# Nine small index tables of the feed-forward part are declared behind the large buffers instead of ahead of them

## The reference

```python
x = x + xattn(ctx, ctx, layernorm(x), ssm_kernel, D, 8)   # 64 heads, causal convolution of length 1024
h = layernorm(x).reshape(-1, 1024)                         # 8192 tokens
scores = sigmoid(h @ router_w)                             # 32 experts, 8 are taken per token
...
gate = ragged_dot(xs, w_gate, group_sizes)                 # (1024 -> 512) per expert
up   = ragged_dot(xs, w_up, group_sizes)
down = ragged_dot(silu(gate) * up, w_down, group_sizes)    # (512 -> 1024)
routed = (down[unsort].reshape(T, 8, 1024) * tkw[..., None]).sum(axis=1)
shared = silu(h @ sw_gate) * (h @ sw_up) @ sw_down         # 1024 -> 1024 -> 1024
x = x + (routed + shared)
```

## The kernel before, in words

| buffer | offset | size | mod 128 |
|---|---|---|---|
| `khi`, `klo`, `thi`, `tlo` (first stage) | 52800 to 142911 | 18432 and 4096 | 64 |
| `raw`, `whi`, `wlo` | 31296, 80448, 129600 | 49152 each | 64 |
| `quad`, `idx`, `xidx`, `gidx`, `yidx` (nine) | 178752 | 32 each, 288 in all | |
| `xg0`, `xg1` | 179040, 183136 | 4096 each | 96 |
| `xhi`, `xlo` | 187232, 191328 | 4096 each | 96 |
| `hb`, `hz`, `hhi`, `hlo` | 195424 | 2048 each | 96 |
| `yrow0`, `yrow1`, `picked0` to `picked3` | 203616 | 4096 each | 96 |

## Time and profile before

### The profile page before, as it was taken

One profiled execution on the slowest core, in us unless ns is written; L12 is line 12 of the kernel. 1 busy time (PEld: TensorE's weight loads), 2 busy tenths in 40 slices (PEclk: granted clock), 3 DMA queues, 4 the chain that ended last, 5 costly groups with the idle time before them and its releaser, 6 DMA issues.

```text
span 13915.1 us, 195311 instructions
## 1 busy us (share of the span) xinstructions
PE 13460.4 (97%) x59424; PEld 10927.4 (79%) x59425; DVE 6480.4 (47%) x7111; ACT 3094.5 (22%) x4072; POOL 6447.4 (46%) x6981
## 2 busy tenths in 40 slices
PE   9999995999999999999999999999999999999999
PEld 7888884888888787887877777787888887887887
DVE  6888885333333333334333334334333334666666
ACT  4444441111111212112121222212111111111111
POOL 6778885333333333333333333333333334555554
PEclk9999997999999999999999999999999999999999
DMA  3444444333333433334333434434333334777777
GB/s 123 117 111 117 114 113 85 94 111 111 94 110 110 126 110 124 93 112 142 96 108 107 129 122 144 139 99 153 94 93 111 94 93 128 250 247 244 250 251 237
DMA packets 935880, 1846.00 MB, mean 133 GB/s; under 512 B 168913, under 2 KB 515921, under 8 KB 909474
## 3 DMA queue, kind: packets, MB, share of 16 engines
q0 software_dynamic: 318976, 892.19, 20.1%
q1 hardware_dynamic: 132898, 599.04, 14.0%
q10 hardware_dynamic: 483840, 352.54, 9.5%
HBM read 1261.41 MB, written 597.54 MB: 134 GB/s over the span
## 4 chain that ended last, share of the span: by engine, by line
PE 78%; DMA 2%; DVE 2%; issue 1%; ACT 0%; DVEq 0%; ACTq 0%; SPq 0%; POOL 0%; POOLq 0%
PE gps L1343 26%; PE ups L1343 26%; PE yps L1343 25%; DMA hsd<-hb 1%; DVE wlo L1254 1%; DMA hz<-hsd 0%; DMA raw<-in_w_gu_dram 0%; DVEq L1053 0%; DVE xlo L1254 0%; ACT xhi L1200 0%; DVE hp L1297 0%; ACT whi L1194 0%; ACTq L1206 0%; DVE yrow L1285 0%; ACTq L1053 0%
## 5 line engine op out<-in xcount | busy, mean ns | idle before, releaser
L1126 POOL DMA_INDIRECT xg<-xnd,xidx x2688 | 2734.1, 1017 | 1204.4 <-issue 632.8
L1166 POOL DMA_INDIRECT yd<-yrow,yidx x544 | 578.9, 1064 | 4707.8 <-DVE yrow L1316 4684.2
L1254 DVE TENSOR_TENSOR xlo<-xt,xhi 128x1024 fp32r<-128x1024 f32 x672 | 822.7, 1224 | 3997.1 <-ACT xhi L1200 3996.6
L1343 PE MATMUL gps<-whi,xhi 128*128 128x512 f32 x5376 | 2133.6, 397 | 213.1 <-DVE xlo L1254 131.8
L1343 PE MATMUL gps<-wlo,xhi 128*128 128x512 f32 x5376 | 2129.3, 396 | 0.0
L1343 PE MATMUL gps<-whi,xlo 128*128 128x512 f32 x5376 | 2128.9, 396 | 0.0
L1343 PE MATMUL ups<-whi,xhi 128*128 128x512 f32 x5376 | 2127.8, 396 | 0.0
L1343 PE MATMUL ups<-wlo,xhi 128*128 128x512 f32 x5376 | 2127.3, 396 | 0.0
L1343 PE MATMUL ups<-whi,xlo 128*128 128x512 f32 x5376 | 2126.7, 396 | 0.0
L1343 PE MATMUL yps<-whi,hhi 128*128 128x512 f32 x5376 | 1701.7, 398 | 117.1 <-DVE wlo L1254 96.8
L1343 PE MATMUL yps<-wlo,hhi 128*128 128x512 f32 x5376 | 1697.9, 397 | 0.0
(11 more groups left out here) (168 smaller groups left out, 17539.3 us busy)
## 6 DMA issues: line engine op xcount, KB each, us to landing
hsd<-hb ACTq DMA_DIRECT2D x2688, 64.0 KB
hz<-hsd ACTq DMA_DIRECT2D x672, 256.0 KB
raw<-in_w_gu_dram SPq DMA_DIRECT2D x136, 1024.0 KB, 7.3
raw<-in_w_dn_dram SPq DMA_DIRECT2D x68, 1024.0 KB, 6.7
kT<-in_ctx_dram SPq DMA_DIRECT2D x64, 704.0 KB, 8.6
xg<-xnd,xidx POOLq DMA_INDIRECT x2688
xin<-in_x_dram SPq DMA_DIRECT2D x64, 512.0 KB
thi<-kph SPq DMA_DIRECT2D x64, 512.0 KB, 5.9
```

Of the source, the lines that this page charges most:

```text
L1126: pool.indirect_dma_start(out=xg[slot][:, q, :], out_offset=None, in_=quarters, in_offset=bass.IndirectOffsetOnAxis(ap=xidx[slot][:, q:q + ...
L1166: pool.indirect_dma_start(out=yd, in_=yrow[i][:, :], in_offset=None, out_offset=bass.IndirectOffsetOnAxis(ap=yidx[i][:, 0:1], axis=0), bou ...
L1254: return dve.tensor_tensor(dst, src, hi.bitcast(F32), ALU.subtract)
L1343: ins = pe.matmul(ps, rows, w[:, chunk, i * 512:(i + 1) * 512], start=first and n == 0, stop=last_one and n == 2)
```

## The change

The nine small tables are declared behind `picked`, the last of the large buffers, and no longer ahead of `xg`. Nothing else in the program differs: each engine has the same instructions in the same order, with the same waits. The offsets of what was behind the tables fall by 288 bytes: `xg`, `xhi`, `xlo`, `hb`, `hz`, `hhi`, `hlo`, `yrow` and `picked` then have residue 64 modulo 128, as `raw`, `whi` and `wlo` do, and also residue 64 modulo 256. `quad`, the first of the nine, goes from 178752 to 227904. All tables keep the residues that they have.

```diff
         raw, w_ld = keep["raw"], keep["w_ld"]
-        quad = sb("quad", [P, QUADS], I32)
-        idx = [sb(f"idx{i}", [P, QUADS], I32) for i in range(2)]
-        xidx = [sb(f"xidx{i}", [P, QUADS], I32) for i in range(2)]
-        gidx = [sb(f"gidx{i}", [P, K // 2], I32) for i in range(2)]
-        yidx = [sb(f"yidx{i}", [P, 1], I32) for i in range(2)]
         xg = [sb(f"xg{i}", [P, QUADS, L // QUADS]) for i in range(2)]
...
         picked = [sb(f"picked{k}", [P, L]) for k in range(K // 2)]
+        quad = sb("quad", [P, QUADS], I32)
+        idx = [sb(f"idx{i}", [P, QUADS], I32) for i in range(2)]
+        xidx = [sb(f"xidx{i}", [P, QUADS], I32) for i in range(2)]
+        gidx = [sb(f"gidx{i}", [P, K // 2], I32) for i in range(2)]
+        yidx = [sb(f"yidx{i}", [P, 1], I32) for i in range(2)]
```

## The result

| | before | after |
|---|---|---|
| median of the timed runs (4 and 4), us | 13980.67 | 13679.46 |
| ratio, with 95% interval | | 0.9782 (0.9768 to 0.9796) |
| profiled execution, us | 13916.77 | 13670.27 |
| first to last feed-forward matmul in the profile, us | 11532.0 | 11220.4 |

The changed kernel is 301 us faster by the medians; the forecast was 309 us and a time of 13,673 us. The two profiled executions differ by 246.5 us only. The feed-forward got 311.6 us shorter in them, and the part ahead of it 65.1 us longer (its first matmul comes at 2434.8 us instead of 2369.7).

A forecast was written before the change was run, and what follows sets the result against it. The prediction took TensorE's feed-forward matmul pace as the bound. It summed 322 - 12 - 1 (half-clock matmuls) = 309 us, so 13982.5 - 309 = 13,673 us, with a stated range of 13,645 to 13,830.

The forecast's parts named there:

- What bounds the kernel: TensorE, busy for 97% of the span; the feed-forward matmuls of line 1343 hold 77% of it.
- Term 1, the pace: Feed-forward: 48,384 matmuls go from 0.23333 to the convolution's 0.22667 us each, saving 322 us.
- The rival that residues don't matter: Feed-forward: addresses don't set the pace, so no change, 13,982 us; chance 0.11.
- the alternation of outputs: Feed-forward: writing two outputs in turn could explain the 0.2333 pace under the no-change rival, 13,982 us; chance 0.11.
- Term 2, what waits give back: Feed-forward: a faster TensorE waits longer for others, giving back 12 us together.
- Part (a): Gate/up: 32 waits for wlo at an expert's first tile grow by 5 us.
- Part (b): Down: 11 waits for wlo, at most 0.48 us longer each, cost 5 us.
- Part (c): 5 waits for hlo, tied to the gate/up of 48 matmuls, cost 2 us.
- Term 3, other engines and transfers: DVE, ACT and transfers on the moved buffers: taken as 0, between 20 us gained and 20 us lost.
- half effect: Feed-forward: address and alternation each hold a part, pace near 0.230 us, saving 160 us, 13,823 us; chance 0.06.
- slower rhythm: Feed-forward at the slowest two convolution steps, 0.235 us each, would lose 82 us; chance of slower 0.05.
- From profile to median: The 309 us gain counted on the profiled execution carries over unchanged to the timed median, 65.8 us higher.

The follow-up runs named there:

- the convolution at (96, 64): Changed kernel with 32 bytes empty ahead of thi and tlo and 224 behind: convolution's stationary operands at residue 96, moving at 64, modulo 256; 13715.8 us, ratio 0.9814.
- the first two kernels of the map: Gaps gave gate/up, down and two convolution buffer slots chosen residue pairs (stationary, moving) modulo 256; 13716.5 and 13640.8 us beside 13908.6 of the kernel before.
- third kernel of the map: Other gap sizes than the first two: gate/up (0, 0), down (192, 0), convolution slots (0, 0) and (0, 64); 13716.7 us beside 13977.7 of the kernel before.

## Why the prediction was right, and what it had wrong

*What bounds the kernel.* Right. The saving per feed-forward matmul appeared in the time almost whole.

*Term 1, the pace.* 0.2267 was predicted and measured (4405 in the window, as the prediction named). The rival that residues don't matter is refuted by the convolution at (96, 64), which took the slower pace with no other change to its loop. That also settles the alternation of outputs: the feed-forward still alternates and has the faster pace. In the place cited in the prediction, the Trainium skill ("TensorE: Matmul & The Clock Gate", section "Step-by-step: what each phase is for") says that the load of the next weights takes no read bandwidth from the running matmul. The measured 0.2267 against 0.2333, by the addresses of the two operands alone, doesn't agree with taking that as independence in time.

The property was named wrongly, though. The prediction said "with `xhi`, `xlo`, `hhi` and `hlo` at residue 64", modulo 128, and compared the convolution by that residue. What counts is equality modulo 256. Here both are met, because the buffers move by 288 = 256 + 32 bytes. In the kernel with 96 bytes of gap they aren't, and it gained 0.2%. The comparison of rows had been between two places that agreed in more than the residue that was compared, and a wrong modulus passed with it. That this change meets the right one too was luck: the same sum would have given that other kernel 13,673 us, and it took 13941.8.

*Term 2, what waits give back.* 12 us were predicted. Part (a), the `wlo` waits in gate/up, grew by 6.4 us of 5. Part (b), the `wlo` waits in down, grew by 0.1 of 5 (96.8 and 96.9), so nothing of what TensorE saves was lost there. Part (c), the `hlo` waits, fell by 3.1 where 2 more were expected. The feed-forward as a whole lost 322.6 - 311.6 = 11 us against the counted saving. 3.4 of them are these waits. The rest are single steps above 0.26 us at restarts and at half clock (280 of them in the trace instead of 249), and steps not yet at the steady pace, neither of which the prediction had beyond 1 us. That 11 came out beside 12 is luck.

*Term 3, other engines and transfers.* 0 predicted. DVE's `xlo` takes 1224 ns before and after, ACT's `xhi` 1026 and 1028. DVE's add into `yrow`, now at 64, still takes the 1221 ns of the earlier trace rows, so the 10 ns between the two rows there weren't the residue's. The kernel with only the row buffers moved has a ratio of 1.000. The transfers' buffers lie 288 bytes lower, not 32; it is the residue that fell by 32.

*The rivals.* No half effect and no slower rhythm at equal residues. A steady pace between the two does exist (0.2292), at a difference of -64, which no row of before had shown. The earlier trace rows had 0.230 us only in passing, over the seven steps from 711.04 to 712.65.

*From profile to median.* The prediction carried the gain over as it is, and it came nearly so: 311.6 us in the profiled feed-forward, 301 us between the medians. The 10 us between these two are not accounted for, since the timed runs of before have no trace. The difference of the profiled executions (246.5 us) would have been the wrong number to compare with.

## What to carry to other kernels

In a dense series of float32r matmuls with a weight load for each, compare the time from start to start at two places of the trace, not the durations; 0.2267 against 0.2333 us for 512 columns was 2.2% of this kernel. Give the stationary and the moving operands one offset modulo 256, by the order of the declarations or a small gap, and check the offsets of the built program: a table of 32 bytes ahead of a large buffer is enough to lose it. Where one place of a kernel is taken as the model for another, change one property there (as with the 32 bytes ahead of `thi`) before the rule is believed. Other types and other shapes of operands were not tried here.

## What the runs showed that was not expected

The pace depends on the difference of the two offsets down to a single element: 4 bytes gave 0.2325 us. The dependence isn't symmetric: a stationary operand 64 bytes above the moving one (modulo 256) gives 0.2333, one 64 bytes below it 0.2292. A difference of 96 was not tried. Why equal offsets are best, and whether both read streams meet in one part of the memory, was not shown; only the differences were.

The mixing, routing and plan ahead of the feed-forward have two lengths: the first feed-forward matmul comes at 2364 to 2372 us in three profiles (before and the first two kernels of the map) and at 2427 to 2448 us in all others but the one with the slower convolution (2473). In the longer case TensorE has short idle times of no named cause, here in the changed kernel's profile (in total, times, longest us), where before has `PE yps L730 <- issue: 0.2, 1, 0.2` and `PE ps L768 <- issue: 6.7, 2, 6.4`:

```profile
PE yps L730 <- issue: 40.8, 36, 3.1
...
PE ps L768 <- issue: 19.6, 8, 2.6
PE y L746 <- issue: 16.5, 12, 2.6
```

Together they are 76.9 us against 6.9. Waits for DVE and ACT that got shorter take some of that back, and 65.1 us remain; 53 of the 76.9 lie in one stretch, from 2180 to 2250 us. The 65.1 us are about as long as the 65.8 us by which the profiled execution of before was shorter than its median. The length doesn't go with the kernel. The kernel before itself took 13908.6 us beside the first two kernels of the map, and 13973 to 13981 us at the median beside all others, and the third kernel of the map, whose convolution is changed in the same places, has the longer one. Those first two kernels and the 13908.6 us come from one chip, on which none of the other experiments ran, so the chip may be what differs; no run tells it apart from chance. What causes it stays open.
